# A Mamba block's scan on one core: the last four turned tiles in their order of use, skip terms ahead of them, the output product in four jobs

## The chip, the cores and the metric

One core of a Trainium2 chip runs the whole program. The metric is device time in microseconds (us); lower is better.

## What is computed

Two batches of 1024 rows of 256 features go through a row filter, a Mamba block and a small attention and FFN branch. In the reference, cut to what matters:

```python
x = x + mamba(keep_largest_rows(x, cond))     # rows by norm
x = x + ffn(attention(x, cond, mask))         # one query per head and batch

# mamba(x): d_inner 512, 16 states
xi, z = split(rmsnorm(x, w) @ in_proj)
xi = silu(causal_conv(xi)); dt, B, C = split(xi @ x_proj)
delta = softplus(dt @ dt_w + dt_b)
h = exp(delta * A) * h + delta * xi * B       # scan over time, per channel and state
y = (sum over states of h * C) + xi * D
return x + (y * silu(z)) @ out_proj
```

The query of the attention is the same for all rows of a batch, so that branch is a chain of small products over a batch's rows; its result is one row per batch, added to all rows at the end.

## The kernel before

Each engine runs a list of its own, written out by hand; semaphores alone tie the lists together. Time is cut into 4 chunks of 512 rows (two per batch). A chunk takes 16 scan steps, one per state, so the steps are n = 0 to 63, and the chunk's 512 channels are four groups m of 128 partitions by 512 times.

In a step, ScalarE writes exp(delta * A) for group m into the PSUM bank `dA[m % 2]` (L1378), GpSimd has written the input product into a ring of four slots (L1535), and VectorE scans the group (L1860). TensorE then turns the state to rows of time (`transposes`, L931): time tile i (128 times, four groups) goes into the bank `hT[i % 2]`, in the order i = 1, 0, 3, 2 (`TURNED`). Turned tiles are scaled by C and summed over the states in two ways. Even tiles: ScalarE scales them into `hc` (`mul_step`, L1388), and TensorE turns them back into the accumulator `yacc` (`reduce`, L640). Odd tiles: VectorE adds them to `yTd` (`mac_step`, L1871); in the last chunk GpSimd adds tile 3, except in the first and the last step, from a copy that ScalarE scales (L1397).

A step has two halves, and between them stand side jobs (table `BESIDE`, half 0 to 31 of a chunk). A job is a product on TensorE into one of the two banks of `pp`, taken in turn in the order of the jobs, and a read of that bank by ScalarE or VectorE. A job waits until the job two before it has been read. In the last chunk (steps 48 to 63) most jobs are the attention of batch 0. There `ATT1` = [28, 29] places job A(1,0), 8 products of x by `u`, and job G(1,0).

After step 63 the last chunk ends as follows. `last_skip` (L1005) adds the skip term xi * D of tile 1 or 3 into a bank of `pp` by four products with a diagonal matrix (L636). The jobs Y(3,1) and Y(3,3) add the turned `yTd` to it (L640 into `pp`). VectorE multiplies each of the four tiles by its gate (`gate_tile`, L1636). The jobs O(3,0) and O(3,1) multiply the gated tiles 0 and 2, and 1 and 3, by out_proj (L669), and VectorE adds them to x (L1682). AP and AT (L687, L694) give a short cut to this chunk's share of the first attention product. Then G(1,1), GT, M, RR, S0, S1 and the rest of the attention of batch 1 follow, each small and each waiting for the one before, then the FFN (`TAIL`). R(3,0) and R(3,1) turn the new x to columns (L718), which S1 needs. `WARM` gives how many products of a unit matrix (L893) are put behind a job, whose result nobody reads: 4 behind AT, 2 behind most jobs of the chain.

## Time and profile before

| | us |
|---|---|
| median of 3 runs | 551.34 |
| lowest, highest | 550.96, 563.08 |
| the profiled execution, whole | 554.95 |
| its span on the core | 553.2 |
| TensorE busy in the span | 467.1 (84%) |
| VectorE | 458.3 (83%) |
| ScalarE | 383.4 (69%) |
| GpSimd | 379.6 (69%) |

A time in the trace counts from the span's start. The profiled execution is 554.95 - 553.2 = 1.75 us longer than its span. The scan steps end at about 488 us and the rest is the tail, in which one engine after the other works. A float32 matmul shows as two records in the trace, and a transpose as one, so "x8" of a product is four matmuls. PEld is the load of a matrix into TensorE, PE the product behind it.

### The profile page before, as it was taken

The page shows a single profiled execution, that of the slowest core. Times are in us where ns is not written, and L with a number is a line of the kernel's source. Part 1 is how long each engine was busy: PE and PEld are TensorE (multiplying, and loading weights), DVE is VectorE, ACT ScalarE, POOL GpSimd, SP SyncE. Part 2 cuts the span into 40 slices and gives each one's busy share as a digit, 9 for nine tenths or more (in the row PEclk, how much of TensorE's full clock was granted, in tenths as well). Part 3 has the DMA queues.
Part 4 walks back from the last instruction along what each step waited for, and adds up shares of the span by engine and source line. Part 5 has one row for each costly group of instructions (what it writes and reads, how often), then busy time and mean ns, then how long its engine had stood idle before and what let it go on. Part 6 is the DMA issues. An engine that isn't in the chain of part 4 may idle for free.

```text
span 553.2 us, 7943 instructions
## 1 busy us (share of the span) xinstructions
PE 467.1 (84%) x2773; PEld 336.6 (61%) x2773; DVE 458.3 (83%) x532; ACT 383.4 (69%) x671; POOL 379.6 (69%) x230
## 2 busy tenths in 40 slices
PE   8967898769858998898789998886897949989992
PEld 6423765446547665765676557555896738877651
DVE  4869899998999799779997997899999988961422
ACT  3675687679977787868877978798768768831210
POOL 5029868866999688839995897599979967610001
PEclk9987899977999999889999999899999977998997
DMA  9331011111102111110021011100210590029004
GB/s 289 122 118 39 39 39 39 38 43 38 31 25 98 39 40 38 41 38 1 40 77 39 38 40 41 39 18 25 74 39 38 172 398 13 1 66 380 1 1 156
DMA packets 18207, 39.40 MB, mean 71 GB/s; under 512 B 1697, under 2 KB 10529, under 8 KB 18162
## 3 DMA queue, kind: packets, MB, share of 16 engines
q1 hardware_dynamic: 18162, 38.84, 20.1%
q8 instruction: 23, 0.38, 0.3%
q14 instruction: 22, 0.18, 0.1%
HBM read 36.61 MB, written 2.23 MB: 70 GB/s over the span
## 4 chain that ended last, share of the span: by engine, by line
PE 42%; DVE 30%; issue 14%; ACT 10%; POOL 3%; DVEq 0%; POOLq 0%; ACTq 0%
DVE scanmem L1860 18%; PE hT L931 8%; DVE yTd L1871 6%; PE pp L576 5%; PE pp L669 4%; PE yacc L640 3%; PE dA L893 2%; ACT dA L1378 2%; PE pp L618 2%; POOL scanmem L1535 2%; PE pp L791 2%; PE yacc L636 1%; DVE yTd L1785 1%; PE pp L632 1%; PE pp L864 1%
## 5 line engine op out<-in xcount | busy, mean ns | idle before, releaser
L1535 POOL TENSOR_TENSOR scanmem<-par,scanmem 128x1024 f32<-128x1024 f32 x128 | 300.5, 2372 | 82.4 <-PE hT L931 63.0
L931 PE MATMUL hT<-con,scanmem 128*128 128x128 f32 x1024 | 163.1, 290 | 59.2 <-DVE yTd L1871 43.1
L1378 ACT ACTIVATE dA<-par,Aneg 128x512 f32<-128x512 f32 x256 | 171.9, 690 | 47.1 <-DVE scanmem L1860 45.7
L931 PEld LDWEIGHTS hT<-con,scanmem 128*128 128x128 f32 x1024 | 120.4, 147 | 114.6 <-DVE yTd L1871 39.6
L1860 DVE TENSOR_TENSOR_SCAN scanmem<-dA,carry,scanmem 128x512 f32<-128x512 f32 x128 | 156.3, 1263 | 11.4 <-ACT dA L1378 10.4
L1860 DVE TENSOR_TENSOR_SCAN scanmem<-dA,scanmem 128x512 f32<-128x512 f32 x128 | 148.8, 1204 | 10.2 <-ACT dA L1378 8.4
L1388 ACT ACTIVATE hc<-hT,CTs 128x512 f32<-128x512 f32 x128 | 86.8, 678 | 30.9 <-PE hT L931 30.7
L640 PE MATMUL yacc<-con,hc 128*128 128x128 f32 x512 | 83.1, 288 | 0.0
L1871 DVE SCALAR_TENSOR_TENSOR yTd<-hT,CTs,yTd 128x512 f32<-128x512 f32 x91 | 66.1, 726 | 9.4 <-PE hT L931 9.2
L640 PEld LDWEIGHTS yacc<-con,hc 128*128 128x128 f32 x512 | 65.8, 151 | 0.0
L576 PE MATMUL pp<-xnT,wi 128*128 128x512 f32 x120 | 58.9, 619 | 2.6 <-DVE par L1659 1.3
L1592 POOL TENSOR_TENSOR par<-xt,hc 128x1024 f32<-128x1024 f32 x1 | 2.3, 2345 | 52.1 <-ACT hc L1450 52.1
L576 PEld LDWEIGHTS pp<-xnT,wi 128*128 128x128 f32 x120 | 21.6, 198 | 21.6 <-issue 19.3
L599 PE MATMUL pp<-xr,diag 128*128 128x512 f32 x72 | 32.9, 592 | 0.0
L669 PE MATMUL pp<-wo,par 128*128 128x256 f32 x128 | 30.8, 397 | 0.5 <-DVE par L1636 0.5
L669 PEld LDWEIGHTS pp<-wo,par 128*128 128x128 f32 x128 | 24.9, 199 | 5.0 <-DVE xt L1682 0.9
L1544 POOL TENSOR_TENSOR yTd<-yTd,xnT 128x512 f32<-128x512 f32 x14 | 18.0, 1285 | 7.8 <-ACT xnT L1397 7.8
L599 PEld LDWEIGHTS pp<-xr,diag 128*128 128x128 f32 x72 | 12.7, 190 | 11.5 <-issue 11.5
L1544 POOL TENSOR_TENSOR yTd<-yTd,sm 128x512 f32<-128x512 f32 x15 | 19.2, 1281 | 0.0
L632 PE MATMUL pp<-dbc,wdt 17*128 17x512 f32 x28 | 15.4, 635 | 1.8 <-DVE xt L1682 1.8
L618 PE MATMUL pp<-par,wx 128*49 128x512 f32 x32 | 14.7, 598 | 0.4 <-DVE par L1622 0.4
L1569 POOL TENSOR_TENSOR par<-par 128x512 f32<-128x512 f32 x12 | 15.0, 1279 | 0.0
(210 smaller groups left out, 530.7 us busy)
## 6 DMA issues: line engine op xcount, KB each, us to landing
scanmem<-brow SPq DMA_DIRECT2D x32, 512.0 KB, 3.7
par<-in SPq DMA_DIRECT2D x1, 4096.0 KB, 17.7
scanmem<-in SPq DMA_DIRECT2D x1, 4096.0 KB, 13.6
xt<-in SPq DMA_DIRECT2D x4, 512.0 KB, 6.7
wi<-in SPq DMA_DIRECT2D x2, 1024.0 KB, 8.0
out<-par SPq DMA_DIRECT2D x3, 512.0 KB, 4.4
aw<-in SPq DMA_DIRECT2D x5, 256.0 KB, 6.5
xr<-in SPq DMA_DIRECT2D x1, 1024.0 KB, 10.2
```

The source lines that it names most:

```text
L576: last = mm(o, win[:, k, col:col + P], xnT[:, k, :], start=k == 0, stop=k == KD - 1)
L599: last = mm(o, dg[:, m, k, :], xr3[:, m, k:k + T], start=False, stop=k == KC - 2, skip_group_check=True)
L618: last = mm(o[0:XW, :], wx[:, m, :], xi(n)[:, m, :], start=m == 0, stop=m == CT - 1)
L640: return mm(o[:, m * P:(m + 1) * P], src, ident, start=False, stop=last, is_transpose=True, skip_group_check=True)
L669: last = mm(o[:, i * DM:(i + 1) * DM], dx(e)[:, m, t0:t0 + P], wo[:, m, :], start=m == 0, stop=m == CT - 1)
L931: last = nc.tensor.transpose(hT[:, i % 2, m * P:(m + 1) * P], hb[:, n % RING, m, i * P:(i + 1) * P], ident)
L1378: A(dA[:, m % 2, :], delta(c)[:, m, :], ACT.Exp, scale=Aneg[:, m * NS + s:m * NS + s + 1]).then_inc(da_ready, 1)
L1388: A(hc[:, e % 2, :], hT[:, 0, :], ACT.Copy, scale=CTs[:, c % 2, i, s:s + 1]).then_inc(mul_done, 1)
L1535: nc.gpsimd.tensor_tensor(hb[:, n % RING, ms, :], dx(c)[:, ms, :], Bb[:, row:row + 1, :].to_broadcast([P, 2, T]), ALU.mult).then_inc(bx_re ...
L1544: nc.gpsimd.tensor_tensor(dst, dst, for_pool(n), ALU.add).then_inc(pool_sum_done, 1)
L1860: V.tensor_tensor_scan(hb[:, n % RING, m, :], dA[:, m % 2, :], hb[:, n % RING, m, :], start, ALU.mult, ALU.add).then_inc(scan_done, 1)
L1871: V.scalar_tensor_tensor(dst, src, cs, dst, ALU.mult, ALU.add).then_inc(mac_done, 1)
```

## The change

It has five parts, all near the end of the scan.

1. `ATT1` goes from [28, 29] to [24, 27]: A(1,0) moves from the first half of step 62 to the first half of step 60, and G(1,0) from the second half of step 62 to the second half of step 61.
2. The skip terms of tiles 1 and 3 move from behind step 63's transposes into the first half of step 63, where step 62's tiles are turned.
3. Step 63's tiles are turned in the order 0, 1, 2, 3. Tiles 0 and 1 go group by group into the two banks of `hT`, groups 0 to 2 ahead of the last scan's end; tiles 2 and 3 go into the two banks of `dA`, which the last step's scans no longer need. VectorE gates tile 0 ahead of the last `mac_step`.
4. O(3,0) and O(3,1) become four jobs of one tile each. The tail's order is now Y1, Y3, O0, AP, O2, AT, O1, O3, R0, G(1,1), R1, GT, M.
5. The four warm products behind AT are gone.

```diff
-ATT1 = [28, 29]
+ATT1 = [24, 27]
...
-    tail += [("Y", last, 1), ("Y", last, 3), ("O", last, 0), ("AP", 1, 0), ("O", last, 1), ("AT", 1, 0), ("G", 1, 1), ("R", last, 0), ("GT", 1, 0),
-             ("M", 1, 0), ("R", last, 1)]
+    tail += [("Y", last, 1), ("Y", last, 3), ("O", last, 0), ("AP", 1, 0), ("O", last, 2), ("AT", 1, 0), ("O", last, 1), ("O", last, 3),
+             ("R", last, 0), ("G", 1, 1), ("R", last, 1), ("GT", 1, 0), ("M", 1, 0)]
...
+LAST_TURNED = (0, 1, 2, 3)
...
-WARM = {**{(name, 1, 0): 2 for name in ("GT", "RR", "PT", "YV", "YT", "VV", "WO")}, ("AT", 1, 0): 4,
+WARM = {**{(name, 1, 0): 2 for name in ("GT", "RR", "PT", "YV", "YT", "VV", "WO")},
...
+        def turned_bank(n, i):
+
+            return dA[:, i - 2, :] if n == NCH * NS - 1 and i >= 2 else hT[:, i % 2, :]
...
-                for i in range(2):
-                    if j:
-                        wait_read(pe, ("Y", e, j + 2 * i))
+                for i in range(1 if e == NCH - 1 else 2):
+                    block = j + 2 * i
+                    t0 = block * P
+                    if block % 2:
+                        wait_read(pe, ("Y", e, block))
                     else:
-                        pe.wait_ge(gated, 2 * e + i + 1)
+                        pe.wait_ge(gated, 2 * e + block // 2 + 1)
...
+            def last_transposes(i, ms):
+
+                n = NCH * NS - 1
+                if i == 0:
+                    pe.wait_ge(mul_done, 2 * n)
+                if i == 1:
+                    pe.wait_ge(pool_mul_done, pool_sums(n - 1))
+                for m in ms:
+                    pe.wait_ge(scan_done, CT * n + m + 1)
+                    last = nc.tensor.transpose(turned_bank(n, i)[:, m * P:(m + 1) * P], hb[:, n % RING, m, i * P:(i + 1) * P], ident)
+                if ms[-1] == CT - 1:
+                    last.then_inc(hT_ready, 1)
...
+                    if n == NCH * NS - 1:
+                        last_skip(1)
                     if n:
                         transposes(n - 1, 0)
+                        if n == NCH * NS - 1:
+                            last_skip(3)
                         transposes(n - 1, 3)
...
             n = NCH * NS
-            last_skip(1)
-            transposes(n - 1, 1)
-            transposes(n - 1, 0)
+            last_transposes(0, (0, 1, 2))
+            last_transposes(1, (0, 1, 2))
+            last_transposes(0, (3,))
+            last_transposes(1, (3,))
             reduce(n - 2, 2)
-            transposes(n - 1, 3)
-            transposes(n - 1, 2)
+            last_transposes(2, (0, 1, 2, 3))
             reduce(n - 1, 0)
-            last_skip(3)
+            last_transposes(3, (0, 1, 2, 3))
             reduce(n - 1, 2)
...
             mac_step(n - 1, 1)
+            gate_even(NCH - 1, 0)
             mac_step(n - 1, 3)
-            gate_even(NCH - 1, 0)
             gate_even(NCH - 1, 2)
```

TensorE in the first half of step 60, before. The rows turn step 59's tile 1, run YT (L748) and turn tile 0:

```order
L931 MATMUL hT<-con,scanmem 128x128 [waits pool_mul_done,scan_done]
L931 MATMUL hT<-con,scanmem 128x128 x3
L748 MATMUL pp<-con,sm 128x16 [waits job_free0,job_free1]
L748 MATMUL pp<-con,sm 128x16
L931 MATMUL hT<-con,scanmem 128x128 [waits mul_done]
L931 MATMUL hT<-con,scanmem 128x128 x3
```

The same place in the changed kernel (L940 is the old L931):

```order
L940 MATMUL hT<-con,scanmem 128x128 [waits pool_mul_done,scan_done]
L940 MATMUL hT<-con,scanmem 128x128 x3
L756 MATMUL pp<-con,sm 128x16 [waits job_free0,job_free1]
L756 MATMUL pp<-con,sm 128x16
L743 MATMUL pp<-u,x1T 128x16 [waits job_free0]
L743 MATMUL pp<-u,x1T 128x16 x7
L940 MATMUL hT<-con,scanmem 128x128 [waits mul_done]
L940 MATMUL hT<-con,scanmem 128x128 x3
```

The eight products of A(1,0) (L743) now stand between YT and the turning of tile 0.

TensorE at the end of step 63, before, from the turning of its tile 0 through both back-turned tiles and the skip term of tile 3 (L636) to the last sum:

```order
L931 MATMUL hT<-con,scanmem 128x128 [waits mul_done]
L931 MATMUL hT<-con,scanmem 128x128 x3
L640 MATMUL yacc<-con,hc 128x128 [waits mul_done]
L640 MATMUL yacc<-con,hc 128x128 x3
L931 MATMUL hT<-con,scanmem 128x128 [waits mac_done]
L931 MATMUL hT<-con,scanmem 128x128 x3
L931 MATMUL hT<-con,scanmem 128x128 [waits mul_done]
L931 MATMUL hT<-con,scanmem 128x128 x3
L640 MATMUL yacc<-con,hc 128x128 [waits mul_done]
L640 MATMUL yacc<-con,hc 128x128 x3
L636 MATMUL pp<-par1,diagD 128x128 [waits job_free0]
L636 MATMUL pp<-par1,diagD 128x128 x3
```

And after, from the first of step 63's transposes (L976) on:

```order
L976 MATMUL hT<-con,scanmem 128x128 [waits scan_done,mul_done]
L976 MATMUL hT<-con,scanmem 128x128 [waits scan_done] x2
L976 MATMUL hT<-con,scanmem 128x128 [waits scan_done,pool_mul_done]
L976 MATMUL hT<-con,scanmem 128x128 [waits scan_done] x2
L976 MATMUL hT<-con,scanmem 128x128 [waits scan_done,mul_done]
L976 MATMUL hT<-con,scanmem 128x128 [waits scan_done,pool_mul_done]
L645 MATMUL yacc<-con,hc 128x128 [waits mul_done]
L645 MATMUL yacc<-con,hc 128x128 x3
L976 MATMUL dA<-con,scanmem 128x128 [waits scan_done] x4
L645 MATMUL yacc<-con,hc 128x128 [waits mul_done]
L645 MATMUL yacc<-con,hc 128x128 x3
L976 MATMUL dA<-con,scanmem 128x128 [waits scan_done] x4
```

The skip term is gone from here, tiles 2 and 3 go to `dA` with a wait for the scan alone, and tile 3 stands behind the back-turning of tile 0.

TensorE in the tail, before, from O(3,0) to the warm products: L669 is the output product, L687 is AP, L694 is AT.

```order
L669 MATMUL pp<-wo,par1 128x256 [waits gated,job_free1]
L669 MATMUL pp<-wo,par1 128x256 x3
L669 MATMUL pp<-wo,par1 128x256 [waits gated]
L669 MATMUL pp<-wo,par1 128x256 x3
L687 MATMUL pp<-par1,wou 32x512 [waits job_free1,job_free0,gated]
L687 MATMUL pp<-par1,wou 32x512 x3
L669 MATMUL pp<-wo,par1 128x256 [waits job_free1]
L669 MATMUL pp<-wo,par1 128x256 x3
L669 MATMUL pp<-wo,par1 128x256 [waits job_free0]
L669 MATMUL pp<-wo,par1 128x256 x3
L694 MATMUL pp<-con,sm 128x16 [waits job_free0]
L694 MATMUL pp<-con,sm 128x16 x3
```

And after:

```order
L675 MATMUL pp<-wo,par1 128x256 [waits gated,job_free1]
L675 MATMUL pp<-wo,par1 128x256 x3
L693 MATMUL pp<-par1,wou 32x512 [waits job_free1,job_free0,gated]
L693 MATMUL pp<-par1,wou 32x512 x3
L675 MATMUL pp<-wo,par1 128x256 [waits gated,job_free1]
L675 MATMUL pp<-wo,par1 128x256 x3
L700 MATMUL pp<-con,sm 128x16 [waits job_free0]
L700 MATMUL pp<-con,sm 128x16 x3
L675 MATMUL pp<-wo,par1 128x256 [waits job_free1]
L675 MATMUL pp<-wo,par1 128x256 x3
L726 MATMUL pp<-con,xt 128x128 [waits job_free1]
L726 MATMUL pp<-con,xt 128x128 x3
```

AP and AT now stand between the output products of single tiles. (One row of O(3,3), which reads like that of O(3,1) but waits for job_free0, stands ahead of the last two and is shown here by this sentence only.)

## Rows read from the trace of the kernel before

**Rows 1.** The timeline at steps 60 and 61: start, us, engine, line, tiles.

```profile
467.08 0.52 PEld L748 LDWEIGHTS pp<-con,sm 128*128 128x128 f32 x4 [0.39 <-issue]
467.44 0.51 PEld L931 LDWEIGHTS hT<-con,scanmem 128*128 128x128 f32 x4
...
469.63 3.61 DVE L1860 TENSOR_TENSOR_SCAN scanmem<-dA,carry,scanmem 128x512 f32<-128x512 f32 x3
...
476.61 0.42 PEld L931 LDWEIGHTS hT<-con,scanmem 128*128 128x128 f32 x4 [0.95 <-DVE scanmem L1860]
```

**Rows 2.** The timeline at steps 62 and 63.

```profile
477.89 1.87 PEld L735 LDWEIGHTS pp<-u,x1T 128*128 128x128 f32 x16
...
479.60 0.94 PEld L931 LDWEIGHTS hT<-con,scanmem 128*128 128x128 f32 x8
...
480.38 0.69 ACT L1388 ACTIVATE hc<-hT,CTs 128x512 f32<-128x512 f32 x1 [0.61 <-PE hT L931]
...
482.14 0.64 PE L742 MATMUL pp<-xt,a_sb 128*32 128x256 f32 x8
...
482.43 2.46 DVE L1860 TENSOR_TENSOR_SCAN scanmem<-dA,carry,scanmem 128x512 f32<-128x512 f32 x2 [0.39 <-ACT dA L1378]
...
485.45 0.41 DVE L1696 COPY sm<-pp 128x256 f32<-128x256 f32 x1
...
485.78 2.45 DVE L1860 TENSOR_TENSOR_SCAN scanmem<-dA,carry,scanmem 128x512 f32<-128x512 f32 x2
```

**Rows 3.** The timeline from the last scan to the last gate.

```profile
487.16 0.69 ACT L1388 ACTIVATE hc<-hT,CTs 128x512 f32<-128x512 f32 x1 [0.18 <-PE hT L931]
...
488.29 0.86 PEld L931 LDWEIGHTS hT<-con,scanmem 128*128 128x128 f32 x8
...
488.98 0.75 DVE L1871 SCALAR_TENSOR_TENSOR yTd<-hT,CTs,yTd 128x512 f32<-128x512 f32 x1 [0.75 <-PE hT L931]
489.42 0.69 ACT L1388 ACTIVATE hc<-hT,CTs 128x512 f32<-128x512 f32 x1 [1.57 <-PE hT L931]
...
490.61 0.47 PEld L640 LDWEIGHTS yacc<-con,hc 128*128 128x128 f32 x4
...
491.15 1.06 PE L636 MATMUL pp<-par,diagD 128*128 128x128 f32 x8
491.36 0.69 DVE L1636 TENSOR_TENSOR par<-yacc,par 128x512 f32<-128x512 f32 x1
...
493.29 1.28 DVE L1636 TENSOR_TENSOR par<-pp,par 128x512 f32<-128x512 f32 x2
```

**Rows 4.** The chain that ended last, in order of time, in the tail.

```profile
494.03 3.72 PE pp L669 x16
497.75 1.00 PE pp L687 x8
...
503.23 0.99 PE dA L893 x8
504.22 0.57 PE pp L742 x8
...
507.91 0.93 PE pp L761 x8
```

**Rows 5.** The timeline at R(3,0) and between M and RR.

```profile
505.41 0.60 ACT L1245 ACTIVATE x1T<-pp 128x512 f32<-128x512 f32 x1 [6.00 <-PE pp L718]
...
507.46 0.19 DVE L1701 TENSOR_TENSOR qD<-pp,con 128x32 f32<-128x32 f32 x1 [2.19 <-PE pp L761]
```

**Rows 6.** Four stretches: PE, PEld, DVE, ACT, POOL busy, then PEclk, DMA.

```profile
463.00:465.00 2.00, 2.00 (x14) 2.00 (x13) 1.18 (x2) 1.83 (x4) 1.15 (x1) 0.66 0.00 0
...
508.00:509.00 1.00, 1.00 (x10) 1.00 (x10) 0.00 (x0) 0.67 (x2) 0.00 (x0) 0.87 1.07 382
509.00:510.00 1.00, 1.00 (x5) 0.97 (x5) 0.00 (x0) 0.15 (x1) 0.00 (x0) 0.50 1.09 388
...
512.00:513.00 1.00, 1.00 (x3) 0.38 (x2) 0.19 (x1) 0.00 (x0) 0.00 (x0) 0.92 0.00 0
```

More of the change, by code:

```diff
@@ L163 @@
 TURNED = (1, 0, 3, 2)
+LAST_TURNED = (0, 1, 2, 3)
 def turned(n, i):
-    return NT * n + TURNED.index(i) + 1
+    return NT * n + (LAST_TURNED if n == NCH * NS - 1 else TURNED).index(i) + 1
 def by_pool(n):
@@ L661, in job_O @@
                     pe.wait_ge(half_ready, 3)
-                for i in range(2):
-                    if j:
-                        wait_read(pe, ("Y", e, j + 2 * i))
-                    else:
-                        pe.wait_ge(gated, 2 * e + i + 1)
-                    t0 = (j + 2 * i) * P
+                for i in range(1 if e == NCH - 1 else 2):
[3 more added lines that the diff above has]
+                        wait_read(pe, ("Y", e, block))
+                    else:
+                        pe.wait_ge(gated, 2 * e + block // 2 + 1)
                     for m in range(CT):
@@ L710, in job_R @@
                 wait_read(pe, ("O", e, j))
+                if e == NCH - 1:
+                    wait_read(pe, ("O", e, j + 2))
                 return turn_rows(o, e, j)
@@ L767, in job_G @@
                     wait_read(pe, ("AT", 1, 0))
-                    wait_read(pe, ("O", NCH - 1, 1))
+                    for i in range(NT):
+                        wait_read(pe, ("O", NCH - 1, i))
                 else:
@@ L949, in reduce, with last_skip @@
                 last.then_inc(red_done, 1)
+            def last_skip(i):
+                job = ("Y", NCH - 1, i)
+                wait_free(job)
+                for m in range(CT):
+                    skip(bank(job), NCH - 1, i, m, m == 0)
+            def last_transposes(i, ms):
[9 more added lines that the diff above has]
+                    last.then_inc(hT_ready, 1)
             def squares_turned(b, dst):
@@ L1004, in _ @@
                         run(job)
-            def last_skip(i):
-                job = ("Y", NCH - 1, i)
-                wait_free(job)
-                for m in range(CT):
-                    skip(bank(job), NCH - 1, i, m, m == 0)
             n = NCH * NS
-            last_skip(1)
-            transposes(n - 1, 1)
-            transposes(n - 1, 0)
+            last_transposes(0, (0, 1, 2))
+            last_transposes(1, (0, 1, 2))
+            last_transposes(0, (3,))
+            last_transposes(1, (3,))
             reduce(n - 2, 2)
-            transposes(n - 1, 3)
-            transposes(n - 1, 2)
+            last_transposes(2, (0, 1, 2, 3))
             reduce(n - 1, 0)
-            last_skip(3)
+            last_transposes(3, (0, 1, 2, 3))
             reduce(n - 1, 2)
@@ L1387, in mul_step @@
                     act.wait_ge(red_done, e - 1)
-                A(hc[:, e % 2, :], hT[:, 0, :], ACT.Copy, scale=CTs[:, c % 2, i, s:s + 1]).then_inc(mul_done, 1)
+                A(hc[:, e % 2, :], turned_bank(n, i), ACT.Copy, scale=CTs[:, c % 2, i, s:s + 1]).then_inc(mul_done, 1)
             def pool_mul_step(n):
@@ L1679, in ev_O @@
                 _, e, j = job
-                for i in range(2):
+                for i in range(1 if e == NCH - 1 else 2):
                     g = e * NT + j + 2 * i
@@ L1868, in mac_step @@
                 dst = yTd[:, c % 2, i // 2, :]
-                src, cs = hT[:, 1, :], CTs[:, c % 2, i, s:s + 1]
+                src, cs = turned_bank(n, i), CTs[:, c % 2, i, s:s + 1]
                 wait_sum(dve, n - 1, i)
```

## The prediction

> **What bounds the kernel now.** I read the table of busy shares first. TensorE and VectorE are both near 84%, so an average decides nothing, and I went to the stretch that the change touches, from step 60 to the start of S0. I read it in the timeline, then in the chain that ended last, then in the windows for TensorE's clock.
>
> Up to the last scan, VectorE sets the pace. From 469.63 us its scans stand back to back, three in 3.61 us [rows 1]. The scans of steps 60 to 63 are then followed by `mac_step`, a small job and the next scans, with one gap of 0.39 us ahead of step 63, which a late exponential of ScalarE ended [rows 2]. The last scan ends at 485.78 + 2.45 = 488.23 us.
>
> Between there and O(3,0) at 494.03 us, three engines hand four tiles to each other. TensorE turns tiles 1 and 0 in one run at 488.29, and VectorE takes tile 1 at 488.98, ScalarE tile 0 at 489.42 [rows 3]. The skip term of tile 3 (1.06 us at 491.15) stands on TensorE ahead of the last back-turned tile. O(3,0) starts when the bank of Y(3,1) has been gated, which is the first of the two gates at 493.29.
>
> From 494.03 on, TensorE is in the chain almost without a break: 3.72 us for O(3,0), 1.00 for AP, the same again for O(3,1) and AT, 0.99 for the warm products, 0.57 for G, until RR at 507.91 [rows 4]. That is 13.88 us from O(3,0) to RR. From RR on both kernels do the same work in the same order, so the sum may end there. (RR is taken where the chain has it.)
>
> **A(1,0) moves into step 60: 1.2 us lost.** This is the term I would overlook from the diff, since the move looks like filling a free place. The job's weights take from 477.89 to the next turning at 479.60, so it pushes TensorE's list by 1.71 us [rows 2]. At its old place the next turning (tiles 0 and 3 of step 61) released ScalarE at 480.38, and ScalarE's queue of two scalings, two small reads and an exponential released the scans of step 63 at 482.43. So 482.43 - 479.60 = 2.83 us lie between that turning and the scans of the next step.
>
> At its new place the same chain hangs behind it. YT's load starts at 467.08, late, because YT waits for ScalarE's read of YV, and the turning behind it starts at 467.44 [rows 1]. With A between them it starts at 467.44 + 1.71 = 469.15, and step 61's scans can start at 469.15 + 2.83 = 471.98. In the trace they start at 469.63 + 3.61/3 = 470.83. VectorE thus waits 471.98 - 470.83 = 1.15 us, and since its scans are back to back from there on, nothing wins this back. A bound from below is 0, if ScalarE's queue is shorter there than the 2.83 us. One from above is the whole 1.71.
>
> **What the old place gives back: 0.4 us.** Without A in step 62 the gap of 0.39 us ahead of step 63 closes [rows 2]. G (0.64 us on TensorE at 482.14) goes to the second half of step 61, where TensorE waits 0.95 us for a scan [rows 1], so it costs nothing. Its copy on VectorE, which held the scans from 485.45 to 485.78, now stands ahead of step 62's last scans, so this 0.33 us only moves. Step 63's first scans start at 482.43 - 0.39 + 0.33 = 482.37, and the last two at 485.78 - 0.33 - 0.06 = 485.39, so the scan ends 0.39 us earlier. Skip terms in step 63's first half (two of 1.06 us) take the place of A and G and finish before the turning of tile 3, which waits for VectorE's `mac_step`. If that cover is missing, they cost up to 2.1 us.
>
> **The end of the scan: 1.0 us gained, with the 0.4 in it.** All times here are as if step 60 had lost nothing. The early transposes need the bank that ScalarE empties at 487.16 + 0.69 = 487.85. Before, a run of four gave its reader a start 488.98 - 488.29 = 0.69 us later, at 0.86/8 = 0.11 us each. Tile 0 is complete with the seventh: 487.85 + 0.69 + 3 x 0.11 = 488.87, against 489.42. Tile 1 is the eighth: 488.98, as before. ScalarE ends tile 0 at 489.56. TensorE turns it back at about 489.6, and as the gate came 491.36 - 490.61 = 0.75 us behind that turning, the gate of tile 0 starts at 490.4, against 491.36. The second `mac_step` (0.75 us with its overlap, about 0.65 net) and the gates of tiles 2 and 1 (1.28/2 = 0.64 each) follow without a gap: 490.4 + 0.65 + 3 x 0.64 from the start of gate 0 ends gate 1 at 492.97. O(3,0) starts 0.04 later at 493.0, against 494.03. If the gates were to wait for tile 3, which now stands behind a back-turned tile, half a us of it goes. If TensorE's missing skip term (1.06) counted in full beside the earlier scan, it would be 1.4.
>
> **The tail to RR: 0.6 us gained.** The halves of O cost what the wholes cost: two of 1.86 for 3.72. Each has AP, AT or another half between it and the next user of its bank, and ScalarE and VectorE read a bank in 0.6 us or less [rows 5], so no read is waited for. The 0.99 us of warm products goes. Two waits come. R(3,1) needs the bank of R(3,0), whose read takes 0.60 and about 0.08 around it [rows 5], while G covers 0.57 of that: 0.11. RR stands directly behind M, whose read starts at 507.46 and takes 0.19 [rows 5], with both hand-overs 0.33; before, R(3,1) lay over it. So 0.99 + 0.04 of issue - 0.11 - 0.33 = 0.59.
>
> **A rule of the Trainium skill on the removed warm products.** The clock fell from 2.4 to 1.2 GHz at about 508.7 and rose at 512.2, although TensorE is busy 1.00 of each us there; what ran ahead of it were GT, M and RR, products with 16 columns [rows 6]. The Trainium skill, page "TensorE: Matmul & The Clock Gate", section "Why this matters for your kernels", says that drops come from idle gaps of about 3 us between bursts. By it the tail, which has no such gap, would keep full clock both with and without the four warm products, and the sum would come out 1.7 us lower (the drop's price, worked out below). The trace disagrees, so I leave the drop in.
>
> **Sum.** 1.15 - 1.03 - 0.59 = -0.47 us. Against the profiled execution, 554.95 - 0.47 = 554.5. That execution is 3.6 us above the median of the runs shown, so the forecast is put on the median: 551.34 - 0.47 = 550.9.
>
> SyncE's loads behind the last turned tile and behind Y(3,3) move with these events, by under 1 us, and have ended by 512 us [rows 6].
>
> **The rivals.**
> - *A(1,0) is free in step 60.* If runs without the profiler have ScalarE ahead of TensorE there, the term of 1.15 vanishes: 551.34 - 1.62 = 549.7. For it speaks that the profiled execution differs by 3.6 us from the median, and no trace here says where. Against it, YT waits for ScalarE in any case.
> - *The clock drop leaves S0.* It lasts (1 - 0.87)/0.5 = 0.26 of the us from 508, three whole us, and (1 - 0.92)/0.5 = 0.16 of that from 512: 3.4 us at half speed, worth 1.7 us [rows 6]. The four dense halves of O now end closer to the thin products. Gone, it gives 550.9 - 1.7 = 549.2.
> - *Slower: A(1,0) meets the half clock.* The clock was at 1.2 GHz for (1 - 0.66)/0.5 x 2 = 1.4 of the two us from 463, thus up to 464.4 [rows 6], three us ahead of A's new place at 467.4. If it comes back later than that, A takes 3.4 us for 1.7 and VectorE waits for the difference: 550.9 + 1.7 = 552.6, slower than before. It decides from a recovery 3 us later. A second drop in the tail, where the warm products were, has the same price and joins this case.
> - *The change does nothing that shows.* If VectorE's seven passes from 488.98 to 494 stay the limit with all their old waits, the first part gains only the scan's 0.39: 1.15 - 0.39 - 0.59 = +0.2, thus 551.5.
>
> **Chances.** Forecast 0.45; A free 0.15; clock drop gone 0.1; slower 0.15; nothing that shows 0.15. The range reaches from the two faster cases, less what a median of three moves, to beyond the slower one: 549.0 to 553.0. A difference under 2%, 11 us, can hardly be told from no change on this kernel, and no case comes near it. Faster by over 2% has 0.01, slower 0.02.
>
> **What would show each step.** In the trace after: a gap of 1 us or more on VectorE ahead of step 61's scans, ended by an exponential (A's price); no gap ahead of step 63's; gate 0 about 2.5 us behind the last scan's end, against 491.36 - 488.23 = 3.1; O(3,0) 5.1 us behind it, against 5.8; O(3,0) to RR in 13.3 us, against 13.88. The prediction is wrong if step 61 starts on time, or if the clock falls more or less than once between step 60 and the FFN.

## The result, and the profile after

The changed kernel takes 557.89 us (median of 20 runs, 552.89 to 565.89) where the kernel before takes 554.85 in the same rounds (20 runs, 550.96 to 564.39). The ratio is 1.0064, with a 95% interval of 1.0033 to 1.0094: slower by 0.6%, some 3.5 us. The ratio leaves out executions over 1.5% slower than the fastest of their kernel, so it is not the quotient of the two medians. The forecast was 0.5 us faster. It stood at 550.9 us, and of the 7.0 us that it missed by, 3.5 lie in the kernel before: its 551.34 came from three executions, where twenty give 554.85. Two more comparisons of the same two kernels gave 1.0026 (0.9987 to 1.0064) and 1.0069 (1.0038 to 1.0100).

The profiled execution of the changed kernel took 565.55 us, with a span of 562.1. Between two executions of one kernel the span moves by up to 13 us (the kernel before: 548.9 to 561.6 us in one comparison). In the profiles the difference lies mostly ahead of step 60, where both kernels run the same code and TensorE's clock falls more or less often: the first 16 steps took 118.1 us in the profile before and 123.1 here. A second profiled execution of the changed kernel had those steps in 118.1 us, and is the one to lay beside before. First lines of the pages of both, busy time and share by engine:

```profile
span 562.1 us, 7934 instructions
PE 476.4 (85%) x2765; PEld 344.2 (61%) x2765; DVE 460.2 (82%) x532; ACT 383.6 (68%) x671; POOL 379.6 (68%) x230
```

```profile
span 553.1 us, 7934 instructions
PE 467.8 (85%) x2765; PEld 337.4 (61%) x2765; DVE 458.4 (83%) x532; ACT 383.5 (69%) x671; POOL 379.8 (69%) x230
```

Before has a span of 553.2 us and 7943 instructions. So **inside the span** the change did nothing that adds up: -0.1 us. That execution took 3.5 us outside its span, where before takes 1.75. **Outside the span** lies the loss that can be shown.

The places of the prediction, in the first profile after. The timeline at steps 60 and 61, where [rows 1] stood:

```profile
475.87 0.52 PEld L756 LDWEIGHTS pp<-con,sm 128*128 128x128 f32 x4 [0.83 <-issue]
...
476.31 1.87 PEld L743 LDWEIGHTS pp<-u,x1T 128*128 128x128 f32 x16
...
478.01 0.95 PEld L940 LDWEIGHTS hT<-con,scanmem 128*128 128x128 f32 x8
...
480.13 1.32 ACT L1405 ACTIVATE dA<-par,Aneg 128x512 f32<-128x512 f32 x2
...
480.88 1.28 DVE L1887 TENSOR_TENSOR_SCAN scanmem<-dA,carry,scanmem 128x512 f32<-128x512 f32 x1 [1.21 <-ACT dA L1405]
```

A(1,0) (L743) stands between YT and the turning, the turning comes at 478.01, and 2.87 us later VectorE starts step 61's scans after a wait of 1.21 us for an exponential. The chain of delays is the one that the prediction drew, with its 2.83 us.

From the last scan to O(3,0), where [rows 3] stood:

```profile
495.40 2.45 DVE L1887 TENSOR_TENSOR_SCAN scanmem<-dA,carry,scanmem 128x512 f32<-128x512 f32 x2
...
497.85 0.86 PEld L976 LDWEIGHTS hT<-con,scanmem 128*128 128x128 f32 x8 [0.58 <-ACT hc L1415]
...
498.98 0.75 DVE L1898 SCALAR_TENSOR_TENSOR yTd<-hT,CTs,yTd 128x512 f32<-128x512 f32 x1 [1.13 <-PE hT L976]
...
500.31 0.69 DVE L1663 TENSOR_TENSOR par<-yacc,par 128x512 f32<-128x512 f32 x1 [0.57 <-PE yacc L645]
...
502.17 1.28 DVE L1663 TENSOR_TENSOR par<-pp,par 128x512 f32<-128x512 f32 x2
```

Gate 0 (L1663 on `yacc`) comes 500.31 - 497.85 = 2.46 us behind the last scan (2.5 forecast, 3.13 before), O(3,0) 5.05 behind it.

The chain that ended last, in the tail, where [rows 4] stood: start, us, what.

```profile
502.90 1.99 PE pp L675 x8
504.90 0.99 PE pp L693 x8
505.89 1.93 PE pp L675 x8
507.82 0.80 PE pp L700 x8
508.62 3.56 PE pp L675 x16
512.18 0.02 issue
512.20 0.49 DVE xt L1709
512.70 0.14 issue
512.83 0.64 PE pp L750 x8
513.47 0.59 PE pp L726 x4
...
514.68 0.54 PE dA L902 x4
515.22 0.89 PE pp L769 x8
516.11 0.02 issue
516.13 0.20 DVE qD L1728
516.34 0.14 issue
516.47 1.04 PE pp L769 x8
```

TensorE's run, unbroken before, is now broken twice: ahead of G(1,1) (L750), which waits for VectorE's read of O(3,3) (0.65 us with the hand-overs; G multiplies the new x that this read writes), and ahead of RR, which waits for the read of M (0.36 us). From O(3,0) to RR the chain has 516.47 - 502.90 = 13.57 us, against 13.88.

All stretches side by side, from the starts of the scans and products in the traces, in us (here RR is its first record, up to 0.15 us ahead of its place in the chain; the expectations below use these numbers too):

| stretch | forecast | before | after | after, second | 
|---|---|---|---|---|
| scans of 60 to scans of 61 | 6.5 | 5.38 | 6.68 | 6.67 |
| 61 to 62 | | 5.79 | 5.82 | 5.94 |
| 62 to 63 | | 5.84 | 5.71 | 5.71 |
| 63 to the end of its scans | | 5.80 | 5.44 | 5.44 |
| end of scans to O(3,0) | 5.1 to 5.2 | 5.80 | 5.05 | 5.05 |
| O(3,0) to RR | 13.15 | 13.74 | 13.54 | 13.54 |
| sum | 41.9 | 42.35 | 42.24 | 42.35 |
| device time less span | as before | 1.75 | 3.45 | 3.5 |

(The forecast of the prediction for O(3,0) to RR is 0.59 less than before.)

### The profile page after: what moved, and what is told of

It reads as the page before. It is cut to its first block, busy times and chain, and to the rows that moved or that the text cites. A ratio compares the mean times of both kernels' runs of the same rounds, so it can differ in the third digit from the quotient of the medians.

```text
span 562.1 us, 7934 instructions
## 1 busy us (share of the span) xinstructions
PE 476.4 (85%) x2765; PEld 344.2 (61%) x2765; DVE 460.2 (82%) x532; ACT 383.6 (68%) x671; POOL 379.6 (68%) x230
## 4 chain that ended last, share of the span: by engine, by line
PE 41%; DVE 26%; issue 14%; ACT 11%; POOL 5%; DVEq 0%; ACTq 0%; POOLq 0%
DVE scanmem L1887 16%; PE hT L940 8%; PE pp L581 6%; DVE yTd L1898 5%; POOL scanmem L1562 4%; PE pp L675 4%; PE yacc L645 3%; ACT dA L1405 3%; PE dA L902 2%; PE pp L637 2%; ACT hc L1415 2%; PE pp L623 2%; PE yacc L641 1%; DVE yTd L1812 1%; PE pp L873 1%
## 5 line engine op out<-in xcount | busy, mean ns | idle before, releaser
L940 PE MATMUL hT<-con,scanmem 128*128 128x128 f32 x1008 | 164.5, 295 | 56.8 <-DVE yTd L1898 41.1
L940 PEld LDWEIGHTS hT<-con,scanmem 128*128 128x128 f32 x1008 | 123.1, 151 | 112.2 <-DVE yTd L1898 36.0
L645 PE MATMUL yacc<-con,hc 128*128 128x128 f32 x512 | 85.3, 294 | 0.0
L645 PEld LDWEIGHTS yacc<-con,hc 128*128 128x128 f32 x512 | 67.6, 154 | 0.2
L581 PE MATMUL pp<-xnT,wi 128*128 128x512 f32 x120 | 60.3, 631 | 3.1 <-DVE par L1686 1.8
L637 PE MATMUL pp<-dbc,wdt 17*128 17x512 f32 x28 | 17.3, 706 | 1.8 <-DVE xt L1709 1.8
```

Of the source, the lines that this page charges most:

```text
L581: last = mm(o, win[:, k, col:col + P], xnT[:, k, :], start=k == 0, stop=k == KD - 1)
L637: return mm(o, wdt[:, m * P:(m + 1) * P], dbc[0:DR + 1, :], start=True, stop=True)
L645: return mm(o[:, m * P:(m + 1) * P], src, ident, start=False, stop=last, is_transpose=True, skip_group_check=True)
L940: last = nc.tensor.transpose(hT[:, i % 2, m * P:(m + 1) * P], hb[:, n % RING, m, i * P:(i + 1) * P], ident)
```

## The experiments

Two theories stood at first. **Span**: the loss is the price of A(1,0) in step 60, larger than its 1.15 us, with less gained in the tail. **Outside**: something that the tail's part changes lengthens what lies behind the span. Beside each kernel stands how many instructions TensorE's list has more or less than before: a float32 matmul counts four, a separate wait one. The change removes four matmuls and adds seven waits: -9. The instruction totals on the profile pages agree for every kernel: 7943 instructions before, 7934 with -9, 7931 with -12, 7939 with -4, 7946 with +3, 7950 with +7.

### Parts alone

Edits, each against before: nothing (the control); `ATT1` alone (part 1); parts 2 and 3 alone; parts 2 to 5, which is the changed kernel with the old `ATT1`.

```diff
# control: none
# part 1 alone
-ATT1 = [28, 29]
+ATT1 = [24, 27]
# parts 2 to 5: the changed kernel with
-ATT1 = [24, 27]
+ATT1 = [28, 29]
# parts 2 and 3: as that, but with the old tail, the output product in two jobs and
+WARM = {... ("AT", 1, 0): 4, ...}
```

> The kernel before, unchanged, as if it were a change. It says how far the order of the states in which the clock of TensorE falls can move a ratio by itself. If the +0.6% of the changed kernel is chance in that draw, this one can be off by as much, some 3 us; if the comparison is sound, the ratio is 1.000 within 0.002, 1 us.

> Part 1 alone: A(1,0) into step 60, G(1,0) into step 61. By the theory that the new place costs (1.15 us lost ahead of step 61, 0.39 gained ahead of step 63) it is 0.8 us slower, up to 3 us if the timed runs meet it in another phase. By the rival that A's products in step 60, beside YT, VV and AX, which are all thin, let the clock of TensorE fall in step 61 (as it did in the changed kernel's trace at 483.2 us), it is 2 us slower or more and the trace shows that fall again. By the rival that all loss lies in the tail, it is 0 to 0.8 us slower.

> The changed kernel with part 1 undone: A(1,0) in step 62 as before, the rest of the change kept. G(1,0) then holds the bank of the skip term of tile 3, which may cost up to 0.5 us. By the theory that A's place is what costs, this is 1.0 to 1.6 us faster than the kernel before, or at least no slower. By the rival that the loss is in the tail or at the scan's end, it is still 2 to 3 us slower.

> Parts 2 and 3 alone: skip terms in step 63, the last tiles by group and into idle banks, gate of tile 0 first; A, G and the tail's jobs as before. By the sum, O(3,0) starts 5.2 us behind the last scan's end where it was 5.8, so 0.6 us faster (less if the skip term waits for G). By the rival that the loss is at the scan's end it is 1 us slower or more.

| kernel | list | ratio to before, 95% | 60 to 61 | scans to O | O to RR | outside span |
|---|---|---|---|---|---|---|
| control | 0 | 0.9998 (0.9968, 1.0027) | 5.38 | 5.79 | 13.75 | 1.75 to 1.84 |
| part 1 | 0 | 1.0041 (1.0005, 1.0077) | 6.67 | 6.06 | 13.74 | 1.75 to 1.84 |
| parts 2, 3 | +3 | 0.9990 (0.9964, 1.0017) | 5.38 | 5.99 | 13.74 | 1.76 to 1.84 |
| parts 2 to 5 | -9 | 1.0019 (0.9988, 1.0050) | 5.38 | 5.99 | 13.54 | 2.89 to 3.98 |

Part 1 costs 1.3 us between steps 60 and 61 and gives 0.5 back by the scan's end. The last scan to O(3,0) is then 0.27 longer, since the skip term of tile 1 still stands ahead of the turning. Its ratio says 2.3 us, with an interval from 0.3, against 0.8 forecast. The fall of the clock that the rival asked for came, at 470.5 us behind A(1,0), but step 61 to 62 took only 5.84 us; another, of 6.8 us from 518.3, came in the tail. Parts 2 to 5 were forecast 1.0 to 1.6 us faster, or 2 to 3 slower by the rival; 1.1 slower was measured, with an interval that holds neither a gain over 0.7 nor a loss over 2.8. In that profile the clock fell at 475.5 and at 482.3 us and step 62 to 63 took 7.09 us, though the code up to there is that of parts 2 and 3, where no fall came and it took 5.84. So such falls come without A(1,0) in step 60 too. The time outside the span follows part 4 or 5, in every one of 12 runs. And parts 2 and 3 alone, forecast 0.6 us faster, do not shorten the scan's end: 5.99 us, longer than before. The timeline of that kernel tells why: VectorE's copy of G(1,0) (L1719), then TensorE's skip term.

```profile
493.42 0.41 DVE L1719 COPY sm<-pp 128x256 f32<-128x256 f32 x1
...
493.88 1.16 PE L641 MATMUL pp<-par,diagD 128*128 128x128 f32 x8 [1.22 <-DVE sm L1719]
...
498.15 0.69 ACT L1411 ACTIVATE hc<-hT,CTs 128x512 f32<-128x512 f32 x1 [1.08 <-PE hT L972]
498.26 0.75 DVE L1894 SCALAR_TENSOR_TENSOR yTd<-hT,CTs,yTd 128x512 f32<-128x512 f32 x1 [2.07 <-PE hT L972]
```

The skip term of tile 3 needs the bank of G(1,0), whose reader stands behind two scans; TensorE waits 1.22 us with step 62's last tiles behind it, and the first reader of step 63's tile 1 comes 0.94 us later than in the changed kernel (2.07 against 1.13 of waiting). So the end's gain and the loss in step 60 belong together: the early skip terms pay only where G has left step 62.

### Is it the length of TensorE's list?

The tail's part changes the order, the jobs and the warm products, and also the length of the list. Behind the tail TensorE's list goes on with code for a general case that these inputs do not need, and ends in a branch over it. If only the length counts, padding must cure it, and shortening before must bring it on. The pads are waits for a semaphore that is long up; two of them in the code make one instruction.

```diff
# e2_after_pad: the changed kernel, at the start of TensorE's list (nine instructions more)
+for _ in range(18):
+    pe.wait_ge(pads_zero, 1)
# e2_before_short: before, without the warm products, seven waits more
-("AT", 1, 0): 4,
+for _ in range(14):
+    pe.wait_ge(pads_zero, 1)
# e2_warm_back: the changed kernel
+("AT", 1, 0): 4,
# e2_tail_only: before with parts 4 and 5
```

> The changed kernel with all five parts; TensorE's list only gets nine more instructions at its start (waits for a semaphore that is long up), which makes it as long as in the kernel before. Theory (the lost time is behind the span: TensorE's code ends at another place, and the end of the program fetches code longer): the time outside the span goes from 3.4 to 4.3 us back to 1.8, and the kernel is about 1.9 us faster than the changed one, ratio to before about 1.000 to 1.003. Rival (the new order of the tail itself makes the end later): still 3.4 to 4.3 us outside the span, ratio about 1.006.

> The kernel before with the four warm products behind AT taken out and seven waits added at the start of TensorE's list: nine instructions shorter than before, as long as in the changed kernel, and nothing else of the change. Theory (place of the code): 3.4 to 4.3 us outside the span instead of 1.8, TensorE's last branch takes about 5.2 us instead of 4.85, ratio about 1.002 (1.9 us behind the span lost, 1.0 us of warm products gained in the chain). Rival (the tail's order): 1.8 us outside the span, ratio about 0.998.

> The changed kernel with the four warm products put back behind AT; TensorE's list is seven instructions longer than in the kernel before. Theory (place of the code): 1.8 us outside the span; warm products cost about 1.0 us in the chain; in sum about 0.9 us faster than the changed kernel. Rival (the tail's order): 3.4 to 4.3 us outside the span and 1.0 us slower than the changed kernel.

> The kernel before with parts four and five of the change alone (four jobs for the output product, no warm products behind AT). TensorE's list is twelve instructions shorter than before. Both theories expect more than 1.8 us outside the span (place of the code: the list is shorter than the changed kernel's, so at least 3.4). O(3,0) to RR takes 13.5 us as in the changed kernel (before 13.74). If the tail itself were worth the 0.59 us that the prediction gave, 13.2.

| kernel | list | ratio to before, 95% | O to RR | outside span |
|---|---|---|---|---|
| after, padded | 0 | 1.0003 (0.9968, 1.0037) | 13.54 | 1.75 to 1.83 |
| before, short | -9 | 1.0005 (0.9978, 1.0033) | 13.18 | 2.84 to 3.96 |
| after, warm products | +7 | 1.0115 (1.0044, 1.0185) | 14.44 | 1.76 to 1.84 |
| before, parts 4 and 5 | -12 | 0.9989 (0.9955, 1.0024) | 13.54 | 3.08 to 3.45 |

The changed kernel has 1.8 us outside its span once its list is as long as before's, and the kernel before has 3.5 once its list is nine shorter. So the length is enough to bring the time on and to take it away; the order of the tail is not needed for it. It does not grow with what is missing: twelve shorter gave 3.1 to 3.45, where at least 3.4 was forecast. The forecast that TensorE's last branch would take 5.2 us in the shortened kernel missed as well: it took 4.98. The expectation for the warm products put back missed: 0.9 us gained was forecast, and the kernel was slower still. It had four runs, and its profile had the clock at half speed for 18 us from RR on where before has 10; but the padded kernel's profile, with a ratio of 1.0003, had 18 us of it too, so why these four were slow was not found. Only the 1.8 us outside the span counts.

Two findings on the way. The whole output jobs without the warm products need 13.18 us to RR, the four jobs 13.54 (13.32 and 13.57 by the chain): **the four jobs cost 0.25 to 0.36 us**, and the gain of the tail's part comes from the removed warm products alone. Their chain in the shortened kernel:

```profile
499.12 3.70 PE pp L669 x16
502.82 0.02 issue
502.84 0.04 DVE xt L1684
502.88 0.36 issue
503.24 0.47 DVE xt L1684
503.72 0.16 DVE a_sb L1693
503.88 0.09 issue
503.97 0.64 PE pp L742 x8
```

Before, 0.80 us of AT and 0.99 of warm products stood between the output product and G(1,1); now 1.15 us of VectorE's reads stand there. The products had covered a wait, so that taking away 0.99 us gives 0.64 at this place, and 0.56 over the chain from O(3,0) to RR (13.32 for 13.88).

### Where is the edge, and can A(1,0) stand elsewhere?

```diff
# e3_after_a25: the changed kernel, nine waits at the start, and
-ATT1 = [24, 27]
+ATT1 = [25, 27]
# e3_best: as e3_after_a25, with the output product in two jobs and the old order of the tail,
#   and thirteen waits at the start instead of nine
# e3_before_m4: before without the warm products, twelve waits at the start
```

> The changed kernel as it is, on the same chip as the next two. Outside the span 3.4 to 4.3 us; VectorE waits 1.2 us ahead of step 61's scans; 5.05 us from the last scan to O(3,0), 13.54 from there to RR. Ratio to before 1.003 to 1.009, of which 1.9 us (0.0034) lie outside the span. If the rest of the loss is part one (A(1,0) in step 60, +1.3 us, less 0.5 in step 63), the span's median is 0 to 1 us above that of before.

> The changed kernel with A(1,0) one half later (ATT1 = [25, 27], the second half of step 60, where TensorE waits for a scan anyway) and nine waits at the start of TensorE's list, so that it is as long as before. Theory (A's 1.3 us come from its place behind YT, and the 1.9 us from the code's place): step 60's scans to step 61's 5.4 to 5.6 us instead of 6.68; outside the span 1.8; in sum 3 us faster than the changed kernel, ratio to before about 0.998 to 1.000. Rival (any A(1,0) in step 60 costs the same, since TensorE is full there): 6.6 us again and about 1.9 us faster than the changed kernel.

> A(1,0) in the second half of step 60 and G(1,0) in that of step 61, the scan's end as in the changed kernel (parts two and three), no warm products behind AT, but the output product as two whole jobs in the tail's old order, and nine waits at the start of TensorE's list. By the landmarks of the runs so far: A free 0, last scan 0.4 earlier, last scan to O(3,0) 5.05 instead of 5.80, O(3,0) to RR 13.18 instead of 13.74, outside the span 1.8: 1.7 us faster than before, ratio about 0.997. If the four output jobs are needed for the early end (the whole O(3,0) then waits for the gate of tile 2), the last term shrinks to zero and the ratio is 0.998 to 1.000.

> The kernel before without the four warm products behind AT and with twelve waits at the start of TensorE's list: four instructions shorter than before instead of nine. If the time outside the span goes by the place of the code, it is either 1.8 us (the edge lies between four and nine instructions less) or 3.4 to 4.3 (between none and four), and nothing between the two; if it goes by something that the warm products did at the end, it is 3.4 to 4.3.

| kernel | list | ratio to before, 95% | 60 to 61 | 61 to 62 | scans to O | outside span |
|---|---|---|---|---|---|---|
| after | -9 | 1.0026 (0.9987, 1.0064) | 6.67 | 5.94 | 5.05 | 3.24 to 3.77 |
| A in half 25 | 0 | 1.0074 (1.0043, 1.0104) | 5.38 | 10.70 | 5.05 | 1.74 to 1.84 |
| the same, two jobs | 0 | 1.0052 (1.0015, 1.0090) | 5.38 | 10.70 | 5.05 | 1.77 to 1.84 |
| before, -4 | -4 | 0.9988 (0.9946, 1.0029) | 5.38 | 5.79 | 5.80 | 1.77 to 1.83 |

Four instructions less change nothing, nine less do: a step, and not a slope. The two kernels with A in half 25 were forecast at 0.998 to 1.000 and 0.997, and both missed. The gain of A in the later half is there (5.38 us from step 60 to 61), and is lost almost four times over one step later (10.70). The timeline of that kernel in step 61:

```profile
471.81 0.97 PEld L769 LDWEIGHTS pp<-yv,aw 128*128 128x128 f32 x8
...
472.71 1.87 PEld L743 LDWEIGHTS pp<-u,x1T 128*128 128x128 f32 x16
...
476.07 0.19 DVE L1752 TENSOR_REDUCE ov<-ovj 128x2 f32<-128x32 f32 x1
...
476.31 3.49 PEld L743 LDWEIGHTS pp<-u,x1T 128*128 128x128 f32 x16 [1.40 <-DVE ov L1752]
...
483.04 2.46 DVE L1889 TENSOR_TENSOR_SCAN scanmem<-dA,carry,scanmem 128x512 f32<-128x512 f32 x2 [2.87 <-ACT dA L1407]
```

and its windows: PE, PEld, DVE, ACT, POOL busy, then PEclk, DMA.

```profile
475.00:476.00 1.00, 0.16 (x2) 0.00 (x0) 0.81 (x2) 1.00 (x2) 1.00 (x1) 1.00 0.00 0
476.00:477.00 1.00, 0.68 (x4) 0.69 (x4) 0.97 (x3) 0.12 (x1) 1.00 (x2) 0.65 0.00 0
477.00:478.00 1.00, 1.00 (x6) 1.00 (x7) 1.00 (x2) 0.00 (x0) 1.00 (x1) 0.50 0.00 0
```

The banks of `pp` are taken in turn in the order of the jobs. VV (L769, read by VectorE) and AX (the second L743; the first is A(1,0)) are jobs of batch 0's attention. The next but one behind VV must wait for VV's read. With A(1,0) in half 24 that was G(1,0), late in step 61; now it is AX, and VectorE ends its reads of VV, queued behind its scans, at 476.26. TensorE stands (1.40 us without a load, 1.16 without a product), and from 476.3 on ((1 - 0.65)/0.5 = 0.7 of that us) the clock is at 1.2 GHz for 6.8 us, so that AX takes 3.49 us for 1.87. The rival of the prediction, a job that meets the half clock, is what happened in this kernel, and with the wait it costs 4.9 us, not 1.7.

### Is the rest inside the span, and is there a better place?

```diff
# e4_best2: parts 2, 3, no warm products, two output jobs, thirteen waits at the start, and
-ATT1 = [28, 29]
+ATT1 = [27, 28]
# e4_before_m4, e4_after_pad, e4_after: the kernels of the sections above, on one chip
```

> The scan's end as in the changed kernel (parts two and three), A(1,0) in the second half of step 61 and G(1,0) in the first half of step 62, whole output jobs in the tail's old order, no warm products behind AT, nine waits at the start of TensorE's list. Theory: TensorE waits 0.95 us for a scan in the second half of step 61, so that A's 1.7 us cost at most 0.8 there, the skip terms of step 63 find their banks free (last scan to O(3,0) 5.05 us, not 5.99), O(3,0) to RR 13.18, outside the span 1.8. From step 60's scans to RR then 28.61 + 13.74 - 0.75 - 0.56 + at most 0.4 net = 41.0 to 41.5 us, against 42.35 before; ratio 0.997 to 0.999. Rival (a job more in step 61 makes the one behind it wait for VectorE's read, as A in step 60's second half did, and the clock falls in that wait): 3 us or more slower there, ratio about 1.005.

> The kernel before without the four warm products behind AT and with twelve waits at the start of TensorE's list: four instructions shorter than before. Outside the span 1.8 us as in its first look, O(3,0) to RR 13.18 instead of 13.74, nothing else: ratio 0.998 to 1.000.

> The changed kernel with nine waits at the start of TensorE's list, now beside the changed kernel itself on one chip. Theory: 1.9 us less outside the span and the same span, ratio to before about 0.0034 lower than that of the changed kernel. Rival (the added waits or another place of the code cost something inside the span too, such as one more fall of the clock in the tail): the span's median is 1 us or more above that of the changed kernel.

> The changed kernel as it is: outside the span 3.4 to 4.3 us, the span's median within 1 us of before's, ratio 1.003 to 1.006.

| kernel | list | ratio to before, 95% | median span | outside span |
|---|---|---|---|---|
| before | 0 | | 553.9 | 1.76 to 1.85 |
| A and G in 27, 28 | 0 | 0.9992 (0.9955, 1.0029) | 553.5 | 1.76 to 1.85 |
| before, -4 | -4 | 1.0018 (0.9982, 1.0054) | 554.1 | 1.75 to 1.85 |
| after, padded | 0 | 1.0020 (0.9984, 1.0055) | 554.8 | 1.76 to 1.85 |
| after | -9 | 1.0069 (1.0038, 1.0100) | 555.4 | 3.40 to 4.02 |

Padded against unpadded differ by 0.0049, 2.7 us, of which 1.9 lie outside the span. The pads had a price of their own, seen in both profiles at the first product on TensorE: it waits for GpSimd's zeros to 1.66 us in the changed kernel, and starts at 2.61 when nine waits stand ahead of it (2.40 with seven, 2.94 with twelve, 3.04 with thirteen). First the changed kernel, then the padded one:

```profile
1.66 6.22 PEld L989 LDWEIGHTS hT<-a_sb 128*128 128x128 f32 x16 [1.66 <-POOL z_sb L1528]
```

```profile
2.61 6.28 PEld L991 LDWEIGHTS hT<-a_sb 128*128 128x128 f32 x16 [2.61 <-issue]
```

The scans began at 44.82 and 45.85 us in the two, and from there the spans are equal within 0.3 us. The medians of the span do not order by what was changed. A and G in halves 27 and 28 missed the forecast of 41.0 to 41.5 us from step 60 to RR: 42.96. The clock fell twice, in steps 61 and 62, and step 62 took 8.07 us. The profile of parts 2 to 5 had two such falls with A and G at their old places, so one profile does not show that the move brought these on. Before without its warm products, four shorter, was forecast at 0.998 to 1.000 and gave 1.0018, within its interval.

### The gains without the losses

The runs so far name three gains: the early turning (0.75 us, if no skip term waits), the missing warm products (0.56), and a list that is not nine shorter. The first needed G gone from step 62 only because of the bank. So A and G stay in step 62, and each skip term goes where its bank is free: tile 1, whose bank A(1,0) leaves, into TensorE's wait of 1.3 us behind step 62's tile 0, and tile 3 right ahead of step 63's tiles. The wait, in the timeline of before:

```profile
485.59 0.66 PE L931 MATMUL hT<-con,scanmem 128*128 128x128 f32 x4 [1.27 <-DVE yTd L1871]
```

```diff
# e5_best3: ATT1 = [28, 29], two output jobs, no warm products behind AT, part 3, and
                     if n:
                         transposes(n - 1, 0)
+                        if n == NCH * NS - 1:
+                            last_skip(1)
...
+            last_skip(3)
             last_transposes(0, (0, 1, 2))
...
+            for _ in range(18):       # behind the last job of TensorE
+                pe.wait_ge(pads_zero, 1)
# e5_after_endpad: the changed kernel with the same loop at the same place
```

> The kernel before (A(1,0) and G(1,0) in step 62 as they were, whole output jobs, the tail's old order), with the last tiles turned as in the changed kernel (part three), the skip term of tile 1 behind the turning of step 62's tile 0, where TensorE waits 1.3 us for VectorE, that of tile 3 where the other stood before, right ahead of step 63's transposes; no warm products behind AT; waits at the very end of TensorE's list, so that it is four instructions shorter than before. Theory: no skip term waits for G(1,0)'s bank any more, last scan to O(3,0) 5.1 to 5.3 us (before 5.80, with the early skip terms 5.99), O(3,0) to RR 13.18 (13.74), outside the span 1.8: 1.1 to 1.3 us less from step 60 to RR (before 42.35), ratio 0.997 to 0.999. Rival (A and G themselves hold the end back): 5.8 or more from the last scan to O(3,0).

> The changed kernel with the nine waits at the end of TensorE's list instead of its start, where they held the first product back from 1.66 to 2.64 us. Theory: outside the span 1.8 us, the first product at 1.66 us again, the span that of the changed kernel: 1.9 us faster than the changed kernel, ratio to before 1.000 to 1.002.

| kernel | list | ratio to before, 95% | step 60 to RR | outside span |
|---|---|---|---|---|
| best3 | -4 | **0.9950 (0.9920, 0.9980)** | 41.06 | 1.75 to 1.90 |
| after, pads at the end | 0 | 0.9995 (0.9954, 1.0037) | 42.23 | 1.82 to 1.90 |

The padded changed kernel is now level with before (556.22 us against 556.11), and its first product starts at 1.66 us. Best3 is faster than before: 554.24 us against 556.11 in the medians. Against the padded changed kernel the two intervals overlap. The skip terms and the end in its timeline (L641, then the run of turnings, then the gates):

```profile
492.42 1.06 PE L641 MATMUL pp<-par,diagD 128*128 128x128 f32 x8
493.85 0.66 PE L936 MATMUL hT<-con,scanmem 128*128 128x128 f32 x4 [0.37 <-DVE yTd L1894]
...
495.66 1.06 PE L641 MATMUL pp<-par,diagD 128*128 128x128 f32 x8
496.55 1.04 PE L972 MATMUL hT<-con,scanmem 128*128 128x128 f32 x8
...
501.55 0.70 PE L674 MATMUL pp<-wo,par 128*128 128x256 f32 x2 [0.47 <-DVE par L1659]
```

Neither skip term waits, and O(3,0) stands 5.06 us behind the last scan's end. That makes 42.35 - 41.06 = 1.29 us. The ratio says 2.8 (1.1 to 4.4), more than the 0.997 to 0.999 forecast, and the medians 1.9. A part of the rest can be the clock: in the five profiled executions that combine two output jobs, no warm products and waits added up to -4 or 0, the stretch from the start of S0 to ScalarE's copy into `z_sb` ran at full clock (12.70 us), where the profiles of the changed kernel and of before have a fall (14.0 to 14.3). But the control of before had 12.70 too and lost it again behind, the shortened kernel had 14.2, and the kernel four shorter, which ran through it at full clock in both its profiles, gave 0.9988 and 1.0018. So this is not shown to belong to the edit.

## Why the prediction was wrong

- **A(1,0) in step 60: right.** 1.15 us worked out, 1.30 measured. The wait sits where it was said, and is ended by an exponential. The rival in which A is free there is ruled out by all eight profiles with A at that place (6.67 or 6.68 us). The clock did fall behind it in all profiled executions of the changed kernel, at 474.5 us in the second one, but A had ended, and only 0.03 to 0.15 us of VectorE's time went. So it fell twice ahead of the FFN, which the prediction had given as a sign of being wrong.
- **The old place gives back 0.4: right.** Steps 62 and 63 took 0.13 and 0.36 less, and the gap ahead of step 63 is gone.
- **The end of the scan: right.** The last scan to O(3,0) took 5.05 us, 5.1 to 5.2 forecast. What the text passed over as "finish before the turning" holds only with G gone: with G in step 62 the early skip terms lengthen the end to 5.99.
- **The tail: half of it.** 0.31 us by the chain for the 0.59 of the sum. The failed step here is "no read is waited for": it went through the banks, and G(1,1) needs not a bank but the new x. VectorE's read of the last output job stands in front of G(1,1) for 0.65 us. R(3,0) hides in that wait and RR loses its cover for 0.36 (0.33 forecast). By terms: -0.99 warm products, +0.65 read, -0.48 for the one back-turning that left the chain, +0.36 ahead of RR, and about +0.15 for longer products. The warm products had been the cover of that read.
- **The clock: no gain.** The fall at S0 stayed in all profiled executions of the changed kernel, as the sum had it.
- **What was not in the sum: the time outside the span.** This is the step that made the direction wrong. The prediction closed its sum at RR, since "from RR on both kernels do the same work in the same order, so the sum may end there". With that it put what lies outside the span, 554.95 - 553.2 = 1.75 us, at no change, without a reason and without counting the lists' lengths. It rose to 3.4 to 4.3 us in 18 of 20 runs (2.4 in two): 1.9 us. Every one of 68 runs of a list nine shorter had 2.4 to 4.3, ten of a list twelve shorter 3.1 to 3.5, and about 300 of lists from four shorter to seven longer 1.74 to 1.90.
- **The level.** The forecast was put on 551.34 us, the median of three executions. In twenty the same kernel has 554.85, which is by itself outside the range of 549.0 to 553.0.
- **What stays open.** 0.64% is 3.5 us with an interval from 1.8 to 5.2, and the three comparisons lie at 3.5, 1.4 and 3.8. The stretch from step 60 to RR gives 0.0 to -0.1 and the outside 1.9. From step 60 to the end of the span the three profiled executions of the changed kernel took 87.8 to 87.9 us, and the two of before 87.7 and 88.1: no loss there. But one of the padded changed kernel took 91.5, with the clock at 1.2 GHz from 487.1 to 490.6, 514.4 to 521.3 and 531.5 to 534.9 us. How often such executions come, in either kernel, was not measured. About 1 us remains that no trace shows; the spans' medians (554.4, 553.6, 555.4 against 553.1, 553.9, 553.9, the first of them worked out as 554.85 - 1.8) move by as much between comparisons through falls of the clock ahead of step 60, and whether the edit makes a fall likelier, ahead of step 60 or behind, was not settled. Nor is it known what the chip does in the added 1.9 us. That it loads code behind the last instruction is argued only: the instruction queues move the same number of packets in both. TensorE's last branch is no witness: it took 4.86 us in an execution of the changed kernel with 3.5 outside, and 5.37 in the end-padded one with 1.9. Nor is the length told apart from the place at which the code behind the tail comes to stand: the pads behind the last job, which move only that code, cured it as well. No list more than seven instructions longer, or between four and nine shorter, was run.

## What to carry to other kernels

Subtract the span from the time of every run before explaining a small loss: a difference that sits outside it is found by no view of the trace, and here it went by the length of one engine's list, so that the instructions that were removed (0.3 us by the chain in the tail) cost more (1.9 us) than they gave. Where jobs take banks in turn, moving one changes whose read every job behind it waits for; write down the reader of each bank, with its queue, before and after the move. Warm products can be covering a wait: what they give back when removed is their time less the read that then stands bare.

## What the runs showed of the hardware

- Nine instructions less in TensorE's list, of which the trace of before has 5,763 run, lengthened the end of the program by 0.6 to 2.5 us, mostly by 1.6 to 2.2, in 68 executions; four less did not. Where in the list the instructions were added, at its start or behind the last job, made no difference to this.
- Nine waits for a semaphore already up, at the start of the list, moved the first product from 1.66 to 2.61 us: about 0.1 us each. Seven, twelve and thirteen (2.40, 2.94, 3.04 us) give the same price.
- The clock fell to 1.2 GHz behind a stretch in which TensorE had been busy for 6.99 of 7 us (the second execution of the changed kernel, at 474.5 us), and also right behind a wait of 1.2 us (A in half 25, at 476.3). It stayed there for 3.4 us and for 6.8 us. The kernel before, with six us of 1.00 from 469 to 475 and waits behind them, has no fall there. The Trainium skill, page "TensorE: Matmul & The Clock Gate", section "Why this matters for your kernels", puts drops down to idle gaps of about 3 us; neither stretch has one, so here the measurement decides against it. Windows of the first case (PE, PEld, DVE, ACT, POOL busy, then PEclk, DMA):

```profile
473.00:474.00 1.00, 1.00 (x12) 1.00 (x11) 1.00 (x2) 0.86 (x2) 1.00 (x2) 1.00 0.00 0
474.00:475.00 1.00, 1.00 (x9) 1.00 (x9) 1.00 (x2) 0.52 (x1) 1.00 (x2) 0.75 0.00 0
```
